# A fifth slot of scan states, low B multiplies between GpSimd's C multiplies, and the second expert layer in one body

## The reference

```python
# layer 0: experts, dense with gates that are zero for two of the four
gates = sum(one_hot(top_k(tokens @ router_w.T + router_b, 2)) * softmax(top values))
hid = gelu(tokens @ fc1_w[e].T + fc1_b[e]);  out += gates[e] * (hid @ fc2_w[e].T + fc2_b[e])
x = x + scale * out
# layer 1: LayerNorm over channels, then, on x_norm and on x_norm reversed in time:
xr, z = split(x_norm @ W_in);  xr = silu(causal conv over 4 taps(xr) + conv_b)
dt = softplus((xr @ W_xproj)[:, :6] @ W_dt + b_dt);  B, C = the other 32 columns
h_t = exp(dt_t * A) * h_(t-1) + (dt_t * xr_t) * B_t;   y_t = sum over states of h_t * C_t
y = (y + xr * D) * silu(z);  out = y @ W_out
x = 0.5 * (out_forward + out_reverse) + x
```

## Time and profile before

| | us |
|---|---|
| median of 3 runs | 6504.09 |
| lowest and highest | 6497.11, 7755.59 |
| the profiled execution | 6514.91 |
| its span, first to last instruction | 6513.1 |
| busy VectorE, TensorE, GpSimd, ScalarE | 5462.6, 5198.4, 4843.2, 4440.9 |
| mean granted TensorE clock | 0.822 |

### The profile page before, as it was taken

How to read it: one execution, slowest core, us unless ns; L and a number is a source line. 1 busy time by engine, 2 the same in 40 slices (tenths; PEclk the granted TensorE clock), 3 DMA queues, 4 the chain that set the end, 5 groups by cost and what they waited for, 6 DMA issues and landing times.

```text
span 6513.1 us, 68858 instructions
## 1 busy us (share of the span) xinstructions
PE 5198.4 (80%) x14285; PEld 1535.2 (24%) x14285; DVE 5462.6 (84%) x4732; ACT 4440.9 (68%) x6729; POOL 4843.2 (74%) x1869
## 2 busy tenths in 40 slices
PE   7868788877888788777888788877877788887787
PEld 6222222222222122222222222221222222222222
DVE  1149888898898978998898988889889988989887
ACT  0447767776777767777677767777677776777675
POOL 0038777787778878787777878888787877788777
PEclk9877788787987878887887779887788878887888
DMA  2046665666666665666666666666667665666665
GB/s 87 24 117 149 163 151 145 164 147 155 158 154 158 161 151 143 167 149 167 144 157 160 147 153 153 157 155 163 146 149 169 149 163 144 158 159 149 157 147 137
DMA packets 426416, 965.27 MB, mean 148 GB/s; under 512 B 56032, under 2 KB 56281, under 8 KB 393032
## 3 DMA queue, kind: packets, MB, share of 16 engines
q1 hardware_dynamic: 426056, 961.49, 61.4%
HBM read 777.18 MB, written 184.11 MB: 148 GB/s over the span
## 4 chain that ended last, share of the span: by engine, by line
PE 32%; DVE 29%; issue 21%; ACT 11%; DMA 3%; POOL 2%; SPq 1%; DVEq 1%; ACTq 1%; POOLq 0%; PEld 0%; PEldq 0%
DVE X L1164 17%; PE ps L662 8%; DVE X L1148 7%; PE ps L626 6%; PE ps L692 6%; ACT ps L933 4%; PE ps L683 4%; DVE ps L1136 2%; ACT L843 2%; DVE hid L1126 2%; PE ps L686 2%; PE ps L601 2%; PE ps L667 2%; DMA y_d<-yf 1%; POOL X L1235 1%
## 5 line engine op out<-in xcount | busy, mean ns | idle before, releaser
L1245 POOL TENSOR_TENSOR X<-X,cR 128x2048 f32<-128x2048 f32 x768 | 3473.7, 4523 | 61.9 <-POOL carry L1243 0.2
L1164 DVE TENSOR_TENSOR_SCAN X<-ps,carry,X 128x512 f32<-128x512 f32 x2688 | 3271.2, 1267 | 282.6 <-ACT ps L933 272.2
L933 ACT ACTIVATE ps<-hi,amat 128x512 f32<-128x512 f32 x2048 | 1383.6, 685 | 1233.4 <-DVE X L1164 1221.9
L1235 POOL TENSOR_TENSOR X<-lo,bR 128x2048 f32<-128x2048 f32 x258 | 1169.4, 4533 | 146.7 <-PE ps L692 80.6
L1148 DVE TENSOR_TENSOR X<-hi,ps 128x2048 f32<-128x2048 f32 x512 | 1160.4, 2266 | 0.0
L692 PE MATMUL ps<-X,red 128*32 128x512 f32 x6144 | 1060.8, 790 | 111.2 <-POOL X L1245 110.3
L662 PE MATMUL ps<-win,w_u 97*128 97x512 f32 (+1 forms) x2080 | 1087.9, 674 | 66.5 <-ACT xf L870 55.9
L626 PE MATMUL ps<-xp,w 96*128 96x512 f32 x864 | 663.1, 870 | 517.1 <-ACT S L914 465.4
L1243 POOL COPY carry<-X 128x4 f32<-128x4 f32 x768 | 143.8, 187 | 1118.7 <-DVE X L1164 1114.9
L933 ACT ACTIVATE ps<-lo,amat 128x512 f32<-128x512 f32 x1026 | 690.7, 677 | 84.2 <-DVE X L1164 52.1
L1126 DVE TENSOR_TENSOR hid<-ps,hid 128x512 f32<-128x512 f32 x432 | 291.7, 677 | 358.8 <-PE ps L633 358.6
(11 more groups left out here) (111 smaller groups left out, 4653.8 us busy)
## 6 DMA issues: line engine op xcount, KB each, us to landing
hi<-hi_d SPq DMA_DIRECT2D x516, 512.0 KB, 8.5
lo<-lo_d SPq DMA_DIRECT2D x516, 256.0 KB, 4.5
bR<-bc_d SPq DMA_DIRECT2D x516, 256.0 KB, 7.3
cR<-bc_d SPq DMA_DIRECT2D x516, 256.0 KB, 10.2
hi_d<-S SPq DMA_DIRECT2D x258, 256.0 KB, 11.0
lo_d<-S SPq DMA_DIRECT2D x129, 256.0 KB, 2.0
y_d<-yf SPq DMA_DIRECT2D x128, 256.0 KB, 10.7
yb<-y_d SPq DMA_DIRECT2D x128, 256.0 KB, 3.6
```

The costliest lines, as they stand in the source:

```text
L933: A_(p_a[i % RING][:, :], dt, ACT.Exp, scale=amat[:, column(i):column(i) + 1]).then_inc(s_exp, 1)
L1164: V.tensor_tensor_scan(h, a, h, 0.0 if head else carry[:, i:i + 1], ALU.mult, ALU.add).then_inc(s_scan, 1)
L1235: G.tensor_tensor(batch(par, s), lo[:, LOW:2 * LOW, :].unsqueeze(1).to_broadcast([P, 2, 2, CH]), quads(bR, par, s), ALU.mult).then_inc(s_b ...
L1245: G.tensor_tensor(batch(par, s), batch(par, s), quads(cR, par, s), ALU.mult).then_inc(s_hc, 1)
```

## The change

1. **Slots.** `SLOTS` is 5. Low batches have slots 3 and 4 for themselves; the four high batches take slots 0, 1, 2, 0 in even bodies and 1, 2, 0, 1 in odd ones. B0(n+1) now waits for S0(n), B1(n+1) for S1(n); the high batches wait for S4, S5 and S3 of n-1 and, the last, for S2(n).
2. **GpSimd's order** is C0 C1 B0 (normalise) C2 B1 C3 C4 C5.
3. **Experts.** Residual, all six products and the bias are in the even body; the odd body has H3 to H5 only. S4 of a body is summed in the next one, with S5.
4. **TensorE's order and banks** are new (`bank_uses`, the body of the tensor block): `hidden` comes after `y_begin(1)` and S0, H3 excepted. D1 is in bank 1, D0 in bank 2. `y_begin(0)` is after U0.
5. **Iterations.** gate_y of the old body 9 to 5, evacuate 9 to 4, make_dt(0) 7 to 6, copy_dt(0) 8 to 7, copy_x2 4 to 6, copy_gates 11 to 9, ln_rstd 9 to 10, copy_out 14 or 16 to 8, gate_hidden to 14, 15, 16, silu_x 19 in both bodies, which waits for U1 before anything else; silu_z takes Z1 first.
6. **SyncE.** B and C are stored before the low rows (`store_bc`, new semaphore `s_bc`), B is loaded at once (`load_b`), C later (`load_c`); the piece of x is loaded in the even body, between `load_b` and `store_low`, once Y2 is ready; `store_x2` comes after `load_low`.

```diff
-SLOTS = 4
+SLOTS = 5
+HIGH_SLOTS = ((0, 1, 2, 0), (1, 2, 0, 1))
 def slot(par, s):
-    return (2 * par + s) % SLOTS
+    return 3 + s if s < LOW else HIGH_SLOTS[par][s - LOW]
+def summed_before(par, s):
+    if s < LOW:
+        return False, s
+    mine = HIGH_SLOTS[par][s - LOW]
+    for b in range(s - 1, LOW - 1, -1):
+        if HIGH_SLOTS[par][b - LOW] == mine:
+            return True, b
+    return False, max(b for b in range(LOW, NB) if HIGH_SLOTS[1 - par][b - LOW] == mine)
-D_BANKS = [("D1", 2), ("D0", 1)]
+D_BANKS = [("D1", 1), ("D0", 2)]
 def bank_uses(odd, next_rev, fin):
+    out = [("OUT", 1)] if fin else []
+    z = [("Z1", 2), ("Z0", 1)] if next_rev else []
     if odd:
+        return (D_BANKS + [("H3", 0)] + out + [("H4", 2), ("H5", 1), ("G3", 2), ("G4", 0), ("U0", 1), ("G5", 2), ("U1", 0)] + z)
+    return (D_BANKS + [("Y2", 0), ("MU", 0)] + out + [("GT", 2), ("VAR", 0), ("H0", 1), ("H1", 2), ("H2", 0),
+                                                       ("G0", 2), ("G1", 0), ("U0", 1), ("G2", 2), ("U1", 0)] + z)
...
 SyncE, body
+                store_bc(n + 1, nxt)
+                if fin and rev:
+                    load_y(0, (img + 1) * NCH, chunk_of(q, rev, odd), n * NB + (LOW + 2))
+                load_b(n + 1, nxt)
+                if not odd:
+                    bank, at = u.at["Y2"]
+                    wait_alone(s_pr[bank], at + 1)
+                    load_piece(nimg, j)
+                store_low(nxt, u)
+                wait_alone(s_exp, n * NT + LOW * BATCH)
+                load_low(n + 1, nxt)
                 if not odd:
                     store_x2(*piece_before(img, j), pc - 1, u)
                 wait_alone(s_hc, n * NB + 1)
-                load_bc(n + 1, nxt)
+                load_c(nxt)
                 store_high(nxt, u)
...
 TensorE, body
                 if odd:
+                    hidden(3, pc, u)
+                    sum_states(n - 1, NB - 2, nxt)
+                    sum_states(n - 1, NB - 1, nxt)
+                else:
+                    residual(u)
+                    for m in range(3):
+                        expert_out(m, u, None)
+                    if before is not None:
+                        sum_states(n - 1, NB - 2, nxt)
+                    expert_out(3, u, None)
+                    expert_out(4, u, None)
+                    if before is not None:
+                        sum_states(n - 1, NB - 1, nxt)
                     expert_out(5, u, None)
                     expert_bias(u)
+                y_begin(1, n, f, par)
+                if not odd:
+                    ln_mean(u)
+                if fin:
+                    finish(u, n - 1, finished(img, q, rev, odd)[2], nxt)
+                sum_states(n, 0, par)
                 if odd:
                     hidden(4, pc, u)
+                    hidden(5, pc, u)
                 else:
+                    gates_transposed(nimg, j, u)
                     ln_var(pc - 1, u)
+                    for m in range(3):
+                        hidden(m, pc, u)
                 sum_states(n, 1, par)
+                rows = 3 if odd else 0
+                gate_rows(rows, u, even)
+                gate_rows(rows + 1, u, even)
+                pe.wait_ge(s_win[par], windows)
+                project(0, par, urev, u)
+                gate_rows(rows + 2, u, even)
+                y_begin(0, n, f, par)
+                project(1, par, urev, u)
+                sum_states(n, 2, par)
+                if nrev:
+                    project_z(1, nxt, u)
+                    project_z(0, nxt, u)
+                sum_states(n, 3, par)
                 project_dt(par, u, ahead)
-                sum_states(n, 4, par)
...
 GpSimd, body
-                for s in range(4):
-                    times_c(n, s, par, rev)
-                    if s == 1 and not odd:
-                        normalise(pc - 1)
+                times_c(n, 0, par, rev)
+                times_c(n, 1, par, rev)
                 times_b(n + 1, 0, nxt)
+                if not odd:
+                    normalise(pc - 1)
+                times_c(n, 2, par, rev)
+                times_b(n + 1, 1, nxt)
+                times_c(n, 3, par, rev)
                 times_c(n, 4, par, rev)
-                times_b(n + 1, 1, nxt)
                 times_c(n, 5, par, rev)
```

More of the change, by code:

```diff
@@ L555, in body @@
                     following = NCH - 1 if not rev else chunk_of(q, rev, odd) - 1
[L556 to L563, removed]
+                    load_y(1, (img + 1) * NCH, following, n * NB + (NB + 1))
             bodies(sp, body)
@@ L670, in project_dt @@
             def project_dt(par, x, u):
-                bank, at = x.at["U1"]
-                pe.wait_ge(s_pf[bank], at + 2)
+                for name in ("U0", "U1"):
+                    bank, at = x.at[name]
+                    pe.wait_ge(s_pf[bank], at + 2)
                 outs = begin(u, "D1"), begin(u, "D0")
@@ L715, in piece @@
                     gate_rows(m, u, u)
-                for m in range(experts):
+            pe.wait_ge(s_ready, 1)
+            with pe.Fori(0, NCH - 1) as j:
+                u = piece_uses(j)
+                first_layer(j, u)
+                residual(u)
+                for m in range(HT):
                     expert_out(m, u, u)
@@ L728, in _ @@
             last_piece, first, second, rest, following = prologue_uses()
-            piece(NCH - 1, last_piece, HT - 1)
-            bank, at = last_piece.at[f"G{HT - 1}"]
-            pe.wait_ge(s_pf[bank], at + 2)
+            first_layer(NCH - 1, last_piece)
+            for m in range(2, HT):
+                gate_rows(m, last_piece, last_piece)
+            for m in (HT - 2, HT - 1):
+                bank, at = last_piece.at[f"G{m}"]
+                pe.wait_ge(s_pf[bank], at + 2)
             for par, u in ((0, first), (1, second)):
@@ L982, in body @@
                         softplus_log(0, n + 1)
-                    if i == 4 and not odd:
-                        copy_x2(u, pc - 1)
+                    if i == 4 and before == 0:
+                        evacuate(n - 1, 0, img * NCH + (NCH - 1 if rev else q * 2 + odd - 1))
                     if i == 5:
@@ L987, in body @@
                         copy_b(n, 0, par)
-                    if i == 7 and not odd:
-                        ln_centred(u, pc - 1)
+                    if i == 6 and not odd:
+                        copy_x2(u, pc - 1)
+                    if i == 7:
+                        copy_dt(0, u, n + 1)
+                        if not odd:
+                            ln_centred(u, pc - 1)
                     if i == 8:
-                        copy_dt(0, u, n + 1)
+                        if before == 1:
+                            copy_out(u)
                         copy_b(n, 1, par)
-                    if i == 9:
-                        if before == 0:
-                            evacuate(n - 1, 0, img * NCH + (NCH - 1 if rev else q * 2 + odd - 1))
-                        if not odd:
-                            ln_rstd(u, pc - 1)
+                    if i == 9 and not odd:
+                        copy_gates(u)
+                    if i == 10 and not odd:
+                        ln_rstd(u, pc - 1)
                     if i == 11:
-                        if not odd:
-                            copy_gates(u)
                         gelu(u, range(3, 6) if odd else range(3))
@@ L1005, in body @@
                         evacuate(n, 1, img * NCH + q * 2 + odd)
-                    if i == (16 if odd else 14) and before == 1:
-                        copy_out(u)
                     if i == 16:
                         copy_b(n, 3, par)
-                    if i == (20 if odd else 19):
+                    if i == 19:
                         silu_x(u, par)
```

128 lines of the change are left out of this document (34 added, 94 removed).

## The result

The changed kernel takes 6813.43 us (median of 4 runs, 6811.24 to 6825.45) against 6500.6 us of the kernel before: ratio 1.0488, 95% interval 1.0467 to 1.0508. The ratio leaves out one run of the kernel before, of 7755.59 us, 19% off the others; 6500.6 is the median with it. The changed kernel is 4.9% slower; 6190 us was forecast, and 6430 was the upper end of the range. The profiled execution has a span of 6809.4 us.

The account below looks back on a forecast made before the run. VectorE was taken as the bound, with holes. Forward 44.3 and reverse 45.0 us a body, mean 44.65: 127 x 44.65 = 5671, plus 477 outside, plus 32, less 3, is 6177; with small additions 6190 us. Range 6050 to 6430.

Parts of the forecast that it names:

- the one on DMA: SyncE's low rows: load_low out at T = 13, landed at 19, B0 due at 19.9; costed at 0.
- rival d: SyncE's wait for Y2 delays load_low by 4 us or more, about 3 us a body come back: 6500 us; chance 0.05.
- Rival (b): VectorE's dBx of batch 5 waits for S2, both U at 1.2 GHz in each body: 6694 us; chance 0.06.
- the cover: Time by which S2 is done before VectorE's batch 5 multiply at T = 35: 0.3 to 1.7 us.
- What would show it: List of trace signs for right or wrong: GpSimd's, TensorE's, VectorE's and ScalarE's waits, and what releases B0.
- (a): TensorE's low clock eats the forward gain and part of the reverse one: 6364 to 6420 us; chance 0.14.
- the removed H waits: TensorE's waits of 3.4 and 3.8 us at hidden(4) and hidden(3) in odd bodies, for a dt copy, go.
- the early y gate: The y gate moves from iteration 9 to 5 and finds its sum within about 1 us.
- the second expert layer: On TensorE, residual and five products, about 0.9 us each, go from odd to even body; no work added.
- the y copy: ScalarE's y copy in iteration 4 holds back copy_b(0) in even forward bodies: 2.3 us a forward pair.
- 4 us in each image's first reverse body: y goes to DRAM and back there: 4 us extra, 8 x 4 = 32 us in the run.
- S3 would start at 1.2 GHz: TensorE idles 4 to 6 us before S3 in forward bodies; S3, D1, D0 then end 7.5 us after C3, not 4.8.

Follow-up runs that it names:

- e5: The changed kernel with the window load of 97 rows split in two, 96 rows and the row of ones: 6121.16 us, 0.9425 of the kernel before.
- e12: e5 with GpSimd's order C0 C1 normalise C2 B0 C3 B1 C4 C5: 6030.67 us, 0.9273 of the kernel before.
- e2: The changed kernel with the window load moved from the head of SyncE's body to behind load_b: 7008.34 us, 1.0732 of the kernel before.

## Why the prediction was wrong

**The step that failed is the one on DMA, "costed at 0".** It reckoned load_low out at T = 13, landed at 19, and B0 due at 19.9. In the odd body shown, whose scan 0 starts at 2842.77, load_low was out at T = 22.7 and landed at 30.4, and GpSimd was ready at 22.4. At the two ends of the loop the low rows came 5.3 and 8.1 us after GpSimd was ready. Three things were wrong in the step.

- *The landing of bc_d was left out.* SyncE waits for it between store_bc and load_b, and store_low stands behind. It took 8.3 us in the median. The rows of the kernel before show bc_d landing in 1.9 us, but there it was issued 11 us after the window load (2640.94 and 2652.18 in that trace); the change moved it to 2.3 us after. I took a duration from a place where it had no neighbour ahead of it and did not ask what it would stand behind.
- *Which wait of SyncE counts.* I named the wait for Y2 (rival d), let it cost about 3 us a body and gave it 0.05. It cost nothing in the changed kernel: SyncE has no row for Y2, and in eight bodies from 2822 on the odd ones, which have no such wait, had the low rows 7.1 to 8.1 us late, the even ones 5.3 to 6.1.
- *It is a loop.* I laid out one body with the low rows' landing as a given. But D1 of the next rows waits for S3, and S3 for C3, which now waits for B0. Lateness is not absorbed by 0.9 us of slack; it sets the period. In e5 the way from bc_d's issue to the low rows' load is 10.3 us in the mean for 16.2, 5.9 less, and the body is 5.4 us shorter (692/127): the period fell until other bounds were met. That is why cutting one DMA in two is worth 692 us.

**Rival (b), the slower one, had the right sign, and in the changed kernel the wrong reason.** Batch 5's multiply does wait for S2, 396 us in all, but in the changed kernel mostly because S2 waited for GpSimd: in 97 of the 124 bodies that can be read, S2 began within 0.1 us of the end of a C multiply. Without the long window load 138 us remain, 1.1 us a body, and most of those are rival (b)'s own mechanism, U0 at the low clock ahead of S2: in e5 the wait comes in all 95 bodies with a U0 of 5.4 us or more, 125 us together, and in one of 23 with 3.70. I had put 0.4 a body; by the prediction's own terms the cover was -0.3 to 1.7 us (35 less 35.3 or 33.3) and not 0.3 to 1.7. This term was 0.7 us too small, some 90 us in the run; the DMA step was the large one.

The signs under "What would show it" did not tell the causes apart, for all three came: batch 5's multiply waits 3.1 us a body (b), ScalarE stands 3.6 us each time for D1 (a), and B0 is released by the lo load (d).

**What the other steps are worth is seen in e5,** which is the changed kernel with one DMA cut in two. The marks of the earlier trace rows, the first dt step of body 0 and of body 127, stand there at

```profile
405.43 0.67 DVE L1149 SCALAR_TENSOR_TENSOR ps<-ps,S 64x512 f32<-64x512 f32 x1
...
6067.78 0.67 DVE L1149 SCALAR_TENSOR_TENSOR ps<-ps,S 64x512 f32<-64x512 f32 x1
```

so a body takes (6067.78 - 405.43)/127 = 44.6 us; the sum of the prediction said 44.65, and its 6190 us is 1.1% over the 6121 measured. By the same marks a forward body takes 44.7 us (44.3 forecast) and a reverse one 44.8 (45.0). Its steps on the removed H waits, on the early y gate and on the second expert layer hold there: VectorE waits 47 us for the gate in the whole run. The closeness of the sum is luck in part. In the fourth image VectorE waits 1.0 (forward) and 1.5 us (reverse) a body for S2, where 0.4 was put, and 0.4 for the y copy in forward bodies, where 1.15 was. The 4 us in each image's first reverse body are not seen either: the step into it takes 42.9 us in the mean.

**The clock.** The prediction said that TensorE would stand before S3 in forward bodies and that S3 would start at 1.2 GHz. It does, in the changed kernel (7.25 us idle, then a granted clock of 0.50) and in e5:

```profile
2755.72 1.06 PE L710 MATMUL ps<-X,red 128*32 128x512 f32 x8
2764.90 1.93 PE L710 MATMUL ps<-X,red 128*32 128x512 f32 x8 [8.12 <-POOL X L1257]
```

The same sum takes 1.93 us after 8.12 us of idle and 1.06 before it, and e5 is faster all the same. S3 and D1 together take 5.1 us in the changed kernel (2842.16 to 2847.25) and 2.95 at the high clock in e12 (3065.00 to 3067.95), so the low clock is some 2 us of the loop's 50.7, an estimate from these rows. The slow U0 accounts for the waits for S2 in e5 and e12, as said above. Neither was measured by an experiment: no run held the clock up.

## What to carry to other kernels

When a step is moved earlier, follow its inputs around the whole loop until they come back to it: a wait with a small cover inside a loop sets the period, and every microsecond is paid in every turn. When a DMA is moved, take its duration from what will stand ahead of it, not from where it stands now, and look at the busy share: 1/16 is one engine at work. When a fix leaves a wait almost as it was, as e12 left S2's, compare the bodies that have it with those that have not. A prime row count can be worth cutting: here 97 rows as 96 and 1 turned a change that lost 4.9% into one that wins 5.8%, although the same cut is worth nothing in the kernel before.

## What the runs showed of the hardware that was not expected

A store issued behind a load that keeps one engine busy lands only about when that load is through (some 8 us, the estimate above): 64 KB took 8.3 us 2.3 us behind a window of 97 rows, 7.8 behind 89, and 1.6 behind 96 rows. The 64 KB store uses more than one engine when it is free: 64 KB in 1.6 us are 40 GB/s, where one engine showed 24 to 26. The 256 KB store of the low rows took 10.3 us behind the B loads and the window load (e2), 5.4 behind the B loads with the window load 12.5 us back (the changed kernel), 3.2 in e5, and 2.0 in the kernel before. And four loads of 256 KB in all that are issued right behind four others of the same size land in 7.6 us, in place of 4.5 when the others went out some 7 us earlier.
